# Products of two neighbouring units of a state scan made one operation behind the even scan

## What is computed

```
def _selective_scan(u, delta, A, Bm, Cm, Dv):
    def step(h, inps):
        u_t, dt, B_t, C_t = inps
        dA = jnp.exp(dt[:, :, None] * A)
        h = dA * h + (dt * u_t)[:, :, None] * B_t[:, None, :]
        y = jnp.einsum('bdn,bn->bd', h, C_t) + Dv * u_t
        return (h, y)
```

## Time and profile before

| | |
|---|---|
| median of 3 runs | 25924.48 us (25921.59 to 25940.24) |
| profiled execution | 25920.02 us, of it 25918.3 us span |
| DVE busy | 23299.7 us, 90% |
| PE busy | 20594.3 us, 79% |
| ACT busy | 12372.3 us, 48% |
| POOL busy | 8447.7 us, 33% |
| DMA | 23.0% of 16 engines in the largest queue |
| one turn of the loop | about 400 us (12276.55 to 12676.34 us in the turn shown) |

### The profile page before, as it was taken

One profiled execution on the slowest core, in us unless ns is written; L12 is line 12 of the kernel. 1 busy time (PEld: TensorE's weight loads), 2 busy tenths in 40 slices (PEclk: granted clock), 3 DMA queues, 4 the chain that ended last, 5 costly groups with the idle time before them and its releaser, 6 DMA issues. The chain is left out here.

```text
span 25918.3 us, 375043 instructions
## 1 busy us (share of the span) xinstructions
PE 20594.3 (79%) x125002; PEld 8874.9 (34%) x125002; DVE 23299.7 (90%) x21779; ACT 12372.3 (48%) x17021; POOL 8447.7 (33%) x4999
## 2 busy tenths in 40 slices
PE   5778878787788887877888878778888787788786
PEld 2333333333333333333333333333333333333332
DVE  5999999999999999899999999999999999999997
ACT  2454444444544444445444454454444444544444
POOL 2333333333333333333333333333333333333331
PEclk8888888888888888888888888888888888888886
DMA  2222222222222222222222222222222222222222
GB/s 74 67 73 65 71 73 63 74 69 67 73 65 71 72 63 74 67 67 74 63 71 72 65 73 68 68 73 64 70 72 64 74 68 67 73 65 71 72 63 63
DMA packets 646792, 1791.26 MB, mean 69 GB/s; under 512 B 76999, under 2 KB 87059, under 8 KB 644760
## 3 DMA queue, kind: packets, MB, share of 16 engines
q1 hardware_dynamic: 624280, 1726.94, 23.0%
q10 hardware_dynamic: 20480, 38.29, 0.5%
HBM read 1707.39 MB, written 44.96 MB: 68 GB/s over the span
## 5 line engine op out<-in xcount | busy, mean ns | idle before, releaser
L1468 POOL TENSOR_TENSOR drive<-du,Bb 128x784 f32<-128x784 f32 x3072 | 5681.0, 1849 | 15616.1 <-DVE drive L1074 15616.1
L457 PE MATMUL scan_sum<-prod,fold 64*64 64x392 f32 x40960 | 6473.1, 596 | 2446.1 <-DVE prod L1074 2426.9
L457 PE MATMUL bank<-pad,dg 64*64 64x392 f32 x59008 | 7746.3, 515 | 171.1 <-POOL dg L1411 98.3
L825 ACT ACTIVATE decay_even<-delta,alog 128x784 f32<-128x784 f32 x3072 | 2816.0, 917 | 9434.8 <-DVE state L1243 9390.8
L1074 DVE TENSOR_TENSOR prod<-state,Cb 128x784 f32<-128x784 f32 x6144 | 6262.4, 1019 | 0.0
L1243 DVE TENSOR_TENSOR_SCAN state<-decay,drive 128x784 f32<-128x784 f32 x3072 | 5825.0, 1896 | 314.9 <-POOL drive L1468 118.2
L1243 DVE TENSOR_TENSOR_SCAN state<-decay_even,drive 128x784 f32<-128x784 f32 x3072 | 5500.5, 1791 | 142.6 <-ACT decay_even L825 33.6
L457 PEld LDWEIGHTS bank<-pad,dg 64*64 64x64 f32 x59008 | 3546.6, 146 | 3994.4 <-issue 3190.7
L457 PEld LDWEIGHTS scan_sum<-prod,fold 64*64 64x64 f32 x40960 | 1732.1, 152 | 5910.1 <-issue 3996.8
L1074 DVE TENSOR_TENSOR drive<-du,Bb 128x784 f32<-128x784 f32 x3072 | 2980.5, 970 | 52.0 <-issue 52.0
L825 ACT ACTIVATE decay<-delta,alog 128x784 f32<-128x784 f32 x3072 | 2865.9, 935 | 2.9 <-DVE delta L1074 1.2
(11 more groups left out here) (175 smaller groups left out, 16623.0 us busy)
## 6 DMA issues: line engine op xcount, KB each, us to landing
Bb<-bc_rows SPq DMA_DIRECT2D x2048, 392.0 KB, 3.7
Cb<-bc_rows SPq DMA_DIRECT2D x2048, 392.0 KB, 4.2
xin<-in_x SPq DMA_DIRECT2D x64, 294.0 KB, 4.3
x_kept<-xin ACTq DMA_DIRECT2D x64, 294.0 KB, 3.7
x<-x_kept SPq DMA_DIRECT2D x64, 294.0 KB, 2.9
out_dram<-t SPq DMA_DIRECT2D x64, 294.0 KB, 2.7
crossed<-pwm ACTq DMA_DIRECT2D x128, 96.0 KB, 2.1
delta<-in_x SPq DMA_DIRECT2D x8, 1176.0 KB, 7.6
```

What stands on the lines that cost most here:

```text
L457: return pe.matmul(out, lhsT, rhs, start=start, stop=stop)
L825: return act.activation(out, in_, f, bias=bias, scale=scale, **more)
L1468: pool.tensor_tensor(drive[:, j % 2, :], du[:, m, :], Bb[:, q % SLOTS, :], ALU.mult).then_inc(drive_r.sem, 1)
```

## The change

Two neighbouring products become one tensor_tensor of 128 x 1568: the state of both units, times the one row of C read twice. It stands behind the scan of the next even unit. So the state needs a ring of three. `prod_ready` counts pairs. PE waits for a pair, sums both units, and only then goes on with other work. The copy of the middle part of the result on ACT (`yk`) moves from j = 66 to j = 68. To make room for the third state, small tiles of the set-up and the 8-bit input of the feed-forward parts (`xq`) move into other buffers.

```diff
@@ block.tensor
             def scan(i, *between):
-                for j, (g, n, k) in enumerate(UNITS):
-                    if j >= 1:
-                        summation(i, j - 1)
-                    go_on(between, j + 1)
+                go_on(between, 1)
+                for j in range(0, NU - 2, 2):
+                    summation(i, j)
+                    summation(i, j + 1)
+                    go_on(between, j + 3)
                 go_on(between, END)
+                summation(i, NU - 2)
                 summation(i, NU - 1)
...
-                pe.wait_ge(prod_r.sem, prod_r.at(i, j + 1))
+                pe.wait_ge(prod_r.sem, prod_r.at(i, j // 2 + 1))
@@ block.scalar
-                    if j == 66:
+                    if j == 68:
                         act.wait_ge(summed.sem, summed.at(i, 64))
@@ block.vector
-                def product(j):
+                def products(j):
                     g, n, k = UNITS[j]
                     q = turn(g, n)
                     v.wait_ge(c_ld[q % SLOTS].sem, c_ld[q % SLOTS].at(i, 16 * (q // SLOTS + 1)))
-                    v.wait_ge(state_r.sem, state_r.at(i, j + 1))
+                    v.wait_ge(state_r.sem, state_r.at(i, j + 2))
                     if j >= PRODS or later(i):
-                        v.wait_ge(summed.sem, summed.at(i, j - PRODS + 1))
-                    tt(prod[:, j % PRODS, :], state[:, j % 2, :], Cb[:, q % SLOTS, :], ALU.mult).then_inc(prod_r.sem, 1)
+                        v.wait_ge(summed.sem, summed.at(i, j - PRODS + 2))
+                    first = j % STATES
+                    pair = state[:, 2::-2, :] if first == STATES - 1 else state[:, first:first + 2, :]
+                    tt(prod[:, j % PRODS:j % PRODS + 2, :], pair, Cb[:, q % SLOTS, :].unsqueeze(1).to_broadcast([128, 2, L]),
+                       ALU.mult).then_inc(prod_r.sem, 1)
...
-                    if j >= 2 or later(i):
-                        v.wait_ge(prod_r.sem, prod_r.at(i, max(j - 1, 0)))
+                    if j >= STATES or later(i):
+                        v.wait_ge(prod_r.sem, prod_r.at(i, (j - STATES) // 2 + 1))
...
-                    if j >= 1:
-                        product(j - 1)
+                    if j >= 2 and j % 2 == 0:
+                        products(j - 2)
                     go_on(between, j)
                     if j % 2 == 1 and j + 1 < NU:
                         driving(j + 1)
                 go_on(between, END)
-                product(NU - 1)
+                products(NU - 2)
```

More of the change, by code:

```diff
@@ L29 @@
 DECAYS = 3
+STATES = 3
 PRODS = 6
@@ L165, in build @@
         seT2 = sb("seT2", [RHID, T0, 128])
-        rT1 = sb("rT1", [C, RHID])
         rT2 = sb("rT2", [RHID, E])
         rb1 = sb("rb1", [RHID, 1])
-        rb2 = sb("rb2", [128, E])
         seb1 = sb("seb1", [RHID, 1])
@@ L185, in build @@
         bdl = sb("bdl", [128, NK])
-        dpA = sb("dpA", [128, 4])
-        dpB = sb("dpB", [64, 4])
         dsum = sb("dsum", [128, 2])
@@ L221, in build @@
         dwo = sb("dwo", [128, M0, HALF])
+        rT1 = dwo[0:C, 2, 0:RHID]
+        rb2, dpA, dpB = dwo[:, 3, 0:E], dwo[:, 4, 0:4], dwo[0:64, 5, 0:4]
         rT2b = dwo[0:RHID, 0:2, :].rearrange("p m l -> p (m l)")[:, 0:E * 128].rearrange("p (e n) -> p e n", e=E)
@@ L242, in build @@
         decay = sb("decay", [128, DECAYS, L])
-        state = sb("state", [128, 2, L])
+        state = sb("state", [128, STATES, L])
         prod = sb("prod", [128, PRODS, L])
@@ L250, in build @@
         yT = [w[0][0:C, :], w[1][0:C, :]]
-        xq = sb("xq", [C, L], F8)
         h16 = work[:, 2:4, :].rearrange("p a l -> p (a l)").bitcast(F16)[:, 0:3 * L].rearrange("p (m l) -> p m l", m=3)
         hq = work[:, 4, :].bitcast(F8)[:, 0:3 * L].rearrange("p (m l) -> p m l", m=3)
+        xq = work[0:C, 4, :].bitcast(F8)[:, 3 * L:4 * L]
         o16 = work[0:C, 5, :].bitcast(F16)[:, 0:L]
@@ L287, in build @@
         even_r, odd_r, yk_r = sig("even_decay", NU // 2), sig("odd_decay", NU // 2), sig("y_kept")
-        drive_r, state_r, prod_r, summed = (sig("drive_ready", NU), sig("state_ready", NU), sig("prod_ready", NU),
+        drive_r, state_r, prod_r, summed = (sig("drive_ready", NU), sig("state_ready", NU), sig("prod_ready", NU // 2),
                                                         sig("summed", NU))
@@ L419, in rows @@
                     if q - 1 >= SLOTS:
-                        sp.wait_ge(prod_r.sem, prod_r.at(i, last_unit(q - 1 - SLOTS) + 1))
+                        sp.wait_ge(prod_r.sem, prod_r.at(i, last_unit(q - 1 - SLOTS) // 2 + 1))
                     elif later(i):
@@ L425, in rows @@
                     src = row(i, 2 * NS - 1)
-                    sp.wait_ge(prod_r.sem, prod_r.at(i, last_unit(2 * NS - 1 - SLOTS) + 1))
+                    sp.wait_ge(prod_r.sem, prod_r.at(i, last_unit(2 * NS - 1 - SLOTS) // 2 + 1))
                     load_c(2 * NS - 1, src)
@@ L1240, in scan @@
                     v.wait_ge(drive_r.sem, drive_r.at(i, j + 1))
-                    if j >= 2 or later(i):
-                        v.wait_ge(prod_r.sem, prod_r.at(i, max(j - 1, 0)))
-                    v.tensor_tensor_scan(state[:, j % 2, :], DP[:, 0:L] if j % 2 == 0 else decay[:, j // 2 % DECAYS, :], drive[:, j % 2, :], 0.0,
+                    if j >= STATES or later(i):
+                        v.wait_ge(prod_r.sem, prod_r.at(i, (j - STATES) // 2 + 1))
+                    v.tensor_tensor_scan(state[:, j % STATES, :], DP[:, 0:L] if j % 2 == 0 else decay[:, j // 2 % DECAYS, :], drive[:, j % 2, :], 0.0,
                                          ALU.mult, ALU.add).then_inc(state_r.sem, 1)
-                    if j >= 1:
-                        product(j - 1)
+                    if j >= 2 and j % 2 == 0:
+                        products(j - 2)
                     go_on(between, j)
@@ L1328, in ffn @@
             def ffn(i, f, at):
-                yield from norm(i, at, 1 + 2 * f, xq[:, :], saturate=False)
+                yield from norm(i, at, 1 + 2 * f, xq, saturate=False)
                 for m in range(3):
```

## The result

The median is 27152.37 us (27139.51 to 27163.04), that of the kernel before on the same chip 25923.03 us. The ratio is 1.047, with an interval of 1.045 to 1.049. The change makes the kernel slower by some 1230 us. The forecast, 27480, was 330 us too high; its direction and its range held. The profiled execution spans 27161.1 us.

What follows compares the result with a forecast made beforehand. VectorE was taken as the bound, with waits for TensorE growing; place costs less gains sum to 24.8 us an image, times 63 is 1562 us on 25920, so 27480 us. The range was 26500 to 28300.

Steps and rivals of the forecast that it cites:

- The bound: VectorE, busy 90% of the span, sets the time; TensorE sets the end of several chains VectorE waits for.
- The pair: VectorE's two products, 1.98 us together, become one wide product of 1.94: 0.04 us a pair, 1.9 us an image gained.
- TensorE's late start: Even-position steps, behind two sums, start 5.3 to 6.7 us after T, the start of their pair's even scan.
- place 1: Position 62, the pointwise convolution on TensorE: starts 4.5 to 5.9 us later, taken as 5.3 an image.
- places 2 and 3: Positions 63.75 and 63.8: new VectorE wait, 2.8 us; positions 67.5 to 70.5, up to the Gram matrix: 4.0 us an image.
- The end of the turn: Position 93.6: TensorE's late step delays ScalarE's last step and the next first scan, 5.2 to 6.6 us, taken as 6.2.
- Places 5 and 6: Position 1.6: 2.5 us; the norm ahead of 49.6 and feed-forward around 58 and 92: together 5.5 us an image.
- GpSimd: At units 10 and 20 a diagonal waits for TensorE, making GpSimd's drive and the odd scan late: 3.0 us an image.
- Less waiting elsewhere: At three VectorE waits behind even units, 0.82 us of product now lies inside the wait: 2.6 us an image less.
- The faster case: Rival: TensorE's late steps had waited anyway, so order costs nothing and waits behind even units shrink: 25440 us, chance 0.07.
- The clock: Rival: coupled sums leave TensorE idle longer, so more work runs at 1.51 us instead of 0.81: 28500 us, chance 0.09.
- The collision of GpSimd's drive with the wide product: Rival: a drive unable to run beside the wide product delays the odd scan 1.8 us: 30300 us, chance 0.04.

Runs made afterwards that it cites:

- e5: The changed kernel with TensorE's even-position steps ahead of both sums and two narrow products behind the even scan instead of the wide one: 25557.17 us, ratio 0.986.
- e1: The changed kernel with one line more: TensorE issues steps due at an even position ahead of the two sums: 25433.98 us, ratio 0.979.
- e7: The changed kernel with GpSimd's diagonal of position 10.7 due at 11.2, behind the drive of unit 13: 27048.50 us, ratio 1.043.
- e9: e1 with GpSimd's diagonal due at 38.1 moved to 39.3, behind the drive of unit 41: 25399.90 us, ratio 0.980.

## Why the prediction held, point by point

**The bound.** Right: VectorE got a little faster and the kernel slower, by waits for TensorE and for ScalarE behind it.

**The pair.** A wide product of 1.82 us beside idle neighbours and 1.93 from start to start; predicted 1.83 and 1.94. VectorE's busy time fell by 107 us, predicted 120. Most stretches with no other work shrink by 0.05 to 0.08 us a pair and not 0.04, and all other stretches together give 2.7 us and not 1.9. In the bare pairs of both traces the products take 1.99 us from start to start before and 1.94 after, and the drive behind them 1.00 and 0.98; the prediction had 1.98 for the first and no change for the second. The 0.075 of the Trainium skill ("Vector Engine (DVE) Microarchitecture Reference", Measured stream behaviour on trn2) agrees with the bare narrow pair of e5, 0.07; in the time of the kernel 0.040 to 0.046 are left of it.

**TensorE's late start.** Predicted between T + 5.3 and T + 6.7. At the four places shown it is T + 6.4 to 6.5: the couple of sums took 2.8 us from start to start, at a granted clock of 0.50. The prediction tied 1.51 us for a sum to idling before it; e1 has a couple behind 2.86 us of idling that takes 0.8 us a sum, so that tie is too simple. I had taken values from the warm end or between for places 1 to 3. At place 1 part of this was made good by the convolution itself, which then follows busy work: from its first row to VectorE's start it is 7.05 us here and was 8.25. Over the 61 turns the convolution starts 5.7 us later and is 0.5 shorter (7.4 for 7.9), which makes 5.2. So +5.3 came out as +5.2 by two errors that cancel. At places 2 and 3 nothing made it good: +3.6 for 2.8, +4.8 for 4.0. Nor has TensorE's stretch at place 3 no gap, as the prediction read it: the 3x3 convolution waits 0.43 us for ScalarE before and 1.23 after.

**The end of the turn.** The step that failed is the sentence "All this moves as a whole". TensorE's and ScalarE's steps did move by 6.3, but ScalarE's idle time under "issue" is not part of what moves: it went from 3.67 us to 1.98 in the turns shown, and from 3.43 to 2.00 in the median: +5.0 for +6.2. With ScalarE earlier, VectorE's own way (sum, wide product, branch, drive), which the prediction had as hidden, is as late as ScalarE's.

**Places 5 and 6.** +3.1 for 2.5, and +4.4 for 5.5.

**GpSimd.** This is the term that was mis-sized most. The mechanism is right at one place (unit 13, +2.4) and doesn't show at the other; e7 shows it by taking it away. And at unit 41 the kernel before had a wait of 1.9 us for GpSimd's drive that is gone in the kernel after, which no step of the prediction asked for. VectorE's waits for the drive grew from 118.2 to 160.7 us in all, and both stretches together give +0.5 us a turn for 3.0. In 37 of the turns the wide product of unit 40 is lengthened there instead, by a drive that has started before it. Why the wait goes, and is back in e1, was not tested.

**Less waiting elsewhere.** Predicted -2.6, from the product that now stands inside a wait, 0.82 each at three places. Measured -4.2 (-2.0 at unit 16, -0.6 at 42, -1.6 at 76 to 80). One reading is that VectorE comes late to such a wait by all that it lost further ahead, 4.1 us by unit 16 in the table, while the chain waited for did not move as much; no run isolates it. These 1.6 us and the 2.5 of the drive are 4.1 us a turn, 260 us of the 330 by which the forecast was high; the other terms together make up the rest.

**The bounds.** The high ends of the prediction's list add up to 36.2 us an image and not 34.7, so to 28200. The stated range, which ends at 28300, lies beyond both sums, and the result is far below.

**The rivals.** The faster case was computed at 25440; it would hold if TensorE's steps could start where they did. e1 makes just this so, by order, and measures 25434; since other terms moved too, that it agrees to 6 us is luck. The clock: TensorE was granted 0.834 of full speed in the mean, against 0.835 before, so the case in which more of its work runs slow did not come. In the couples of sums at the places above it is in play all the same, as the high ends had it: 2.89 us at 0.50, and 1.55 at 1.00 in e1. The collision of GpSimd's drive with the wide product is there too, in small: in the kernel after, wide products take 3.25 us at unit 22 (in 24 turns), 2.50 at 40 (in 37), 2.63 at 44 and 2.12 at 66 (in all), with a drive or a diagonal running when they start, some 2 us a turn in all. The narrow products of before are lengthened likewise, at seven units. e7 and e9 brought the collision about at one more place each, where the product took 1.4 and 0.6 us longer in the mean of the turns. Each is below the 1.8 that I had set.

## What to carry to other kernels

Before two outputs of the bound engine are joined, look at what stands behind their consumer in its queue: the later of the two now releases every step there, and a step that waits for neither has to be put ahead of both. One line of order was worth 1720 us here, fourteen times what the joined instruction gave. And when costs at single places are summed, follow the engine through the turn: what it loses early it can get back at a later wait, and what a repair gives at one unit can be lost at the next.

## What the runs showed of the hardware

VectorE's products and GpSimd's operations with inputs in SBUF kept each other out, whichever came second. A diagonal beside an even scan takes 0.75 us (e9: DVE, then POOL):

```profile
12221.45 1.79 DVE L1248 TENSOR_TENSOR_SCAN state<-decay_even,drive 128x784 f32<-128x784 f32 x1
```

```profile
12221.89 0.75 POOL L1416 TENSOR_SCALAR_AFFINE_SELECT dg<-kern 128x640 f32<-128x640 f32 x1 [2.99 <-PE bank L456]
```

Started 0.16 us behind a wide product it took 2.30 and ended 0.62 us after it (e1 above). A wide product started 0.16 us behind a GpSimd drive of 1.85 took 3.34: the drive's remainder and its own 1.83 make 3.5. The Trainium skill has this rule, for a VectorE instruction with two inputs in SBUF and a GpSimd one that reads SBUF ("SBUF — State Buffer", Who interferes with whom), and these rows agree with it. It also fits that the even scan, whose decay comes from PSUM, takes 1.79 us beside a drive that starts in the same moment, and the odd one, with decay and drive in SBUF, 2.15 behind a diagonal. What I had not expected is who pays: with one product for two, GpSimd. Its diagonals grew from 1512 to 1842 ns in the mean, and in e1, against e5 with the narrow products, from 1385 to 1983.

A step of ScalarE with nothing but "issue" ahead of it, at the loop's branch, idled 3.4 us in the median of one kernel's turns and 2.0 to 2.1 in the others. Such an idle time isn't a fixed price.
